# Places of float32r operands modulo 256 bytes in a three-stage kernel (MoE, state space, MoE)

## The reference

```python
x = x + 0.5 * ffn(layernorm(x))     # stage a
x = x + mamba(layernorm(x))         # stage m, which adds its own input too
x = x + 0.5 * ffn(layernorm(x))     # stage b, the same weights as stage a
```

## Time and profile before

| | |
|---|---|
| Runs of the kernel | 2362.97, 2363.86 and 2365.33 us, median 2363.86 |
| The profiled execution, from its first to its last instruction | 2361.8 us |
| TensorE busy with matmuls | 2295.3 us, 97% |
| TensorE busy loading weights | 2023.3 us, 86% |
| VectorE, ScalarE, GpSimd busy | 1371.3, 884.1, 690.8 us |
| Mean granted TensorE clock | 0.992 |

### The profile page before, as it was taken

How to read it: one execution, slowest core, us unless ns; L and a number is a source line. 1 busy time by engine, 2 the same in 40 slices (tenths; PEclk the granted TensorE clock), 3 DMA queues, 4 the chain that set the end, 5 groups by cost and what they waited for, 6 DMA issues and landing times.

```text
span 2361.8 us, 41282 instructions
## 1 busy us (share of the span) xinstructions
PE 2295.3 (97%) x16412; PEld 2023.3 (86%) x16412; DVE 1371.3 (58%) x3200; ACT 884.1 (37%) x1562; POOL 690.8 (29%) x534
## 2 busy tenths in 40 slices
PE   6999999999998999999999999999999999999997
PEld 6999998777788888888888888888999999777786
DVE  6767662222228777777777777778776763222221
ACT  5232221233327455554455555455322221233221
POOL 1244442112220332332332223231144444122121
PEclk9999999999999999999999999999999999999999
DMA  8876433989844111111111111104386622889948
GB/s 268 265 244 225 138 102 142 310 271 280 235 91 137 37 29 36 28 28 28 28 28 28 28 28 28 29 20 170 123 289 199 213 82 78 303 275 282 287 82 177
DMA packets 129279, 334.73 MB, mean 142 GB/s; under 512 B 24450, under 2 KB 45186, under 8 KB 118400
## 3 DMA queue, kind: packets, MB, share of 16 engines
q1 hardware_dynamic: 80592, 236.63, 28.2%
q0 software_dynamic: 48496, 95.46, 17.8%
HBM read 218.25 MB, written 172.77 MB: 166 GB/s over the span
## 4 chain that ended last, share of the span: by engine, by line
PE 87%; DMA 6%; DVE 4%; ACT 1%; issue 1%; DVEq 0%; POOL 0%; SPq 0%; ACTq 0%; POOLq 0%
PE m_p_ab L1666 4%; PE m_p_ab L1667 4%; PE m_p_ab L1668 4%; PE m_p_x L1668 3%; PE m_p_x L1667 3%; PE m_p_x L1666 3%; DMA out<-b_y,b_row_no 3%; PE p_up_a L757 3%; PE p_gate_a L757 3%; PE p_gate_a L758 2%; PE p_gate_a L759 2%; PE m_p_y L1786 2%; PE p_up_a L759 2%; PE p_up_a L758 2%; PE m_p_y L1787 2%; PE p_out_a L757 2%
## 5 line engine op out<-in xcount | busy, mean ns | idle before, releaser
L1982 DVE SCALAR_TENSOR_TENSOR m_xt<-m_ssm,m_convw,m_xt 128x256 f32<-128x256 f32 x384 | 219.0, 584 | 58.1 <-ACT m_ssm L1533 48.8
L495 POOL DMA_INDIRECT slot_rows<-a_hr,a_slot_now x128 | 128.3, 1002 | 147.0 <-PE p_gate_a L759 94.0
L495 POOL DMA_INDIRECT slot_rows<-b_hr,b_slot_now x128 | 128.5, 1004 | 146.2 <-PE p_gate_b L759 93.6
L1666 PE MATMUL m_p_ab<-m_ht_hi,m_wi_b_hi 128*128 128x256 f32 x576 | 161.5, 280 | 3.3 <-ACT m_ssm L1533 3.3
L1668 PE MATMUL m_p_ab<-m_ht_hi,m_wi_b_lo 128*128 128x256 f32 x576 | 159.6, 277 | 0.0
L1667 PE MATMUL m_p_ab<-m_ht_lo,m_wi_b_hi 128*128 128x256 f32 x576 | 159.5, 277 | 0.0
L757 PE MATMUL p_gate_a<-a_hts_hi,a_w_hi 128*128 128x256 f32 x512 | 150.2, 293 | 5.2 <-DVE a_hts_lo L1056 5.1
L757 PE MATMUL p_gate_b<-b_hts_hi,b_w_hi 128*128 128x256 f32 x512 | 148.0, 289 | 3.3 <-DVE b_hts_lo L1056 3.2
L1439 POOL TENSOR_TENSOR m_state_dec<-m_state,m_etot 128x1024 f32<-128x1024 f32 x31 | 74.0, 2387 | 255.2 <-ACT m_etot L1549 255.2
L757 PE MATMUL p_up_a<-a_hts_hi,a_w_hi 128*128 128x256 f32 x512 | 147.2, 288 | 0.0
L757 PE MATMUL p_up_b<-b_hts_hi,b_w_hi 128*128 128x256 f32 x512 | 147.1, 287 | 0.0
(11 more groups left out here) (376 smaller groups left out, 7372.3 us busy)
## 6 DMA issues: line engine op xcount, KB each, us to landing
a_ew<-in_ew SPq DMA_DIRECT2D x32, 1536.0 KB, 7.1
b_ew<-in_ew SPq DMA_DIRECT2D x32, 1536.0 KB, 7.2
after_ffn<-a_zeros POOLq DMA_DIRECT2D x6, 2048.0 KB, 9.3
out<-b_zeros POOLq DMA_DIRECT2D x6, 2048.0 KB, 10.2
slot_rows<-a_zeros POOLq DMA_DIRECT2D x1, 8336.0 KB, 39.6
a_rows<-slot_rows SPq DMA_DIRECT2D x32, 260.5 KB, 8.2
b_rows<-slot_rows SPq DMA_DIRECT2D x32, 260.5 KB, 8.2
m_x<-after_ffn SPq DMA_DIRECT2D x16, 512.0 KB, 3.6
```

Of the source, the lines that this page charges most:

```text
L495: g_.indirect_dma_start(out=xg, out_offset=bass.IndirectOffsetOnAxis(ap=slot_now[r % HR][:, at:at + 1], axis=0), in_=hr[r % HR][:, j, :], ...
L1666: t.matmul(out, l_hi, r_hi_, start=first, stop=False)
L1982: ins_ = v.scalar_tensor_tensor(xt[:, m, :], ssm[:, m, i:i + BM], convw[:, m, i:i + 1], xt[:, m, :], ALU.mult, ALU.add)
```

## The change

`Region` gets two arguments, `like` and `past`: a tile with them is moved up to the next place whose offset modulo 256 bytes is that of `like` plus `past`. With them, and with `HS_AT` and `ROUTED_AT` moved up by 96 and then 96 more bytes, streamed operands of 256 columns (`hts_hi`, `hts_lo`, `ht_hi`, `ht_lo`) lie 192 bytes past their weights modulo 256, which is to say the weights 64 bytes past them. The operands of products with 512 columns (`act_hi`, `act_lo`, `htr_hi`, `htr_lo` and `r_both`, `y_hi0`, `y_lo0`) lie at the same offset modulo 256 as their partners, and so do `wi_a_hi` and `wi_a_lo` with the shared weights' start. No instruction, wait or DMA is added, removed or moved in order; the tiles that follow a moved one get other addresses too.

```diff
-HS_AT = SHARED_AT + 4 * CI * (CONV - 1 + BM)
-ROUTED_AT = HS_AT + 4 * (10 * 1024 + 5 * TILES + 6 * TR)
+HS_AT = SHARED_AT + 8384
+ROUTED_AT = HS_AT + 41792
+LINE = 256
...
-    def __call__(self, name, shape, dt=F32):
+    def __call__(self, name, shape, dt=F32, like=None, past=0):
...
+        if like is not None:
+            self.next += (like + past - self.next) % LINE
         at = self.next
...
+        w_at, gap = c.first_byte, LINE - 64
...
-        hts_hi[0], hts_lo[0] = sb("hts_hi0", [P, KD, BS], F32R), sb("hts_lo0", [P, KD, BS], F32R)
+        hts_hi[0], hts_lo[0] = sb("hts_hi0", [P, KD, BS], F32R, w_at, gap), sb("hts_lo0", [P, KD, BS], F32R, w_at, gap)
...
-        hts_hi[1], hts_lo[1] = sb("hts_hi1", [P, KD, BS], F32R), sb("hts_lo1", [P, KD, BS], F32R)
-        act_hi, act_lo = sb("act_hi", [P, 2, 2, BS], F32R), sb("act_lo", [P, 2, 2, BS], F32R)
+        hts_hi[1], hts_lo[1] = sb("hts_hi1", [P, KD, BS], F32R, w_at, gap), sb("hts_lo1", [P, KD, BS], F32R, w_at, gap)
+        act_hi, act_lo = sb("act_hi", [P, 2, 2, BS], F32R, w_at), sb("act_lo", [P, 2, 2, BS], F32R, w_at)
...
-        r_both = rt("r_both", [P, KD, 2, E], F32R)
+        r_both = rt("r_both", [P, KD, 2, E], F32R, w_at)
...
-        htr_hi, htr_lo = rt("htr_hi", [P, 2, BR], F32R), rt("htr_lo", [P, 2, BR], F32R)
+        htr_hi, htr_lo = rt("htr_hi", [P, 2, BR], F32R, w_at), rt("htr_lo", [P, 2, BR], F32R, w_at)
...
-        wi_a = sb("wi_a_hi", [P, KD, SPLIT_COL - NH], F32R), sb("wi_a_lo", [P, KD, SPLIT_COL - NH], F32R)
+        w_at, gap = c.first_byte, LINE - 64
+        wi_a = (sb("wi_a_hi", [P, KD, SPLIT_COL - NH], F32R, w_at), sb("wi_a_lo", [P, KD, SPLIT_COL - NH], F32R, w_at))
...
-        ht_hi, ht_lo = sb("ht_hi", [P, KD, BM], F32R), sb("ht_lo", [P, KD, BM], F32R)
+        ht_hi, ht_lo = sb("ht_hi", [P, KD, BM], F32R, w_at, gap), sb("ht_lo", [P, KD, BM], F32R, w_at, gap)
+        sb.next += (w_at - sb.next) % LINE
...
+        sb = Region(nc, "m", c.first_byte + HS_AT)
         x[2], x[1] = sb("x2", [P, TM, D]), sb("x1", [P, TM, D])
```

## The result

The changed kernel takes 2340.4 us (median of 4 runs, 2337.7 to 2346.2), the kernel before 2363.4 us (median of 4): ratio 0.9907, 95% interval 0.989 to 0.9924. The forecast was 2327.5 us, with 2321 to 2334 us as its own range and 2311 to 2341 us as the outer one. The sign is right; 23 us came in place of 36.4, outside the forecast's own range and just within the outer one. The profiled execution spans 2337.9 us against 2361.8.

What follows compares the result with a forecast made beforehand. TensorE was taken to set the pace, except beside the experts and in the tail, where the adds' queue does. Savings 14.0 + 2.9 + 5.2 + 14.3 = 36.4 us from 2363.9 gave 2327.5 us, range 2321 to 2334, outer 2311 to 2341.

Steps and rivals of the forecast that it cites:

- That place counts, and the period of 256 bytes: All placed products: weights minus streamed operand, modulo 256 bytes, sets the distance of matmul starts; 64 suits 256 columns, 0 suits 512.
- The step of 114.0 ns for gate and up: Gate and up, runs of 48 between two down groups: mean step 114.0 ns, saving taken as 5.7 ns each.
- `wi_a` at 4.6 ns each: Stage m: 60 of a block's 72 wi_a products save 4.6 ns each, most of the 5.2 us for 16 blocks.
- `down` at 6.2 ns, `out_product` j = 0 at 2 ns: Products of 512 columns: down saves 6.2 ns each (bounds 5 and 7.3), out_product with j = 0 about 2 ns.
- The router's 7 ns: Stage a's 64 router products, mean 402 ns, go towards 391: some 7 ns each, 0.4 us in all.
- Stage a before the adds, 14.0 us: Units 1 to 39 with their downs and the router products save 10.7, 2.9 and 0.4 us, as TensorE sets the pace.
- The experts' stretch, put at a gain of 0: Beside the routed experts the adds set the pace; TensorE's 5.6 us are earned and given back in each stage.
- The tail at 0: End of stage b: blocks 14 and 15 would earn 2.9 us, the queue of adds cancels all but a fraction.
- Half: Rival, 10%: runs of 24 too short for the short pace, gate and up gain 2 ns, not 5.7; 2343 us.
- Everything counts: Rival, 10%: adds go faster with TensorE, so experts, tail and fourth part count too; 51.4 us gained, 2312 us.

## Why the prediction was right and wrong

- **That place counts, and the period of 256 bytes: right.** `wi_b` stayed at 277 ns though its rows moved by 256, and the cases at 256 and 320 bytes were as those at 0 and 64. The rule of the Trainium skill (TensorE: Matmul & The Clock Gate, Part 2, step 1), of two independent read ports, doesn't carry over to these products: 120.0 against 113.3 ns by the distance alone, with nothing else running.
- **The step of 114.0 ns for gate and up: this step failed.** The prediction put it as "(6 x 118 + 42 x 113.4) / 48 = 114.0 ns", six longer steps after which every run goes short. The rows it came from, 5 steps of 118 and then 113.4, were those of one entry into `wi_b`. Behind `down` with act at distance 0 nearly every run stays at 117.8 ns to its end (54 of 56; with TensorE alone 6 of 6). Measured: 116.5 ns, a saving of 3.2 in place of 5.7. The change put `down` at the distance where it is fastest itself, and that shuts gate and up out of their short pace; with act moved, 114.7 ns was measured.
- **`wi_a` at 4.6 ns each: the same failure.** 30 of its runs, all behind `out_product`, stayed at 117.8 ns (before 118.2). Stage m gained 2.6 us in place of 5.2.
- **`down` at 6.2 ns, `out_product` j = 0 at 2 ns: right.** Measured 5.5 for `down`, and 228.3 to 227.5 over both halves of `out_product`, some 1.5 for the one. The router's 7 ns were 3 (402 to 399). With hts alone undone, some 5 us are left for all of these.
- **Stage a before the adds, 14.0 us: 6.5.** TensorE's busy time fell by 8.4 us; most of what is missing is the pace above. 1.8 us more went into idle time, for which the sum had no term: TensorE now asks sooner for the router's rows, 8.3 us of waits in place of 6.2.
- **The experts' stretch, put at a gain of 0 because "The adds themselves do not change": right in part, and this step failed too.** The adds do go one after the other whatever TensorE does, and with TensorE 24 us less busy nothing was gained. But their transfers took 3.5 and 3.2 us less in the two stages (237.6 to 234.1 us in stage a). TensorE earned 3.8 us here, by the pace above, and not 5.6; 3.6 of them were kept, and the wait before block 14 stayed at 3.7 us in place of 9. The two errors are of opposite sign, so the total is nearer the forecast than its largest term.
- **The tail at 0: nearly right.** 1.2 us was gained behind block 10 of stage b. The last matmul came 27.5 us earlier, the last block add landed 23.9 us earlier, and the end came 23.9 us earlier, as it does if that queue sets the end.
- **The rivals.** "Half" was the nearest, at 2343 us and 10%: its size was right, its reason (runs of 24 too short) was not: more than half of the runs of 24 of gate and up did get short, of those of 48 behind `down` nearly none. "Everything counts" had a grain of truth in the adds, worth 3 us a stage; in stage b little of it reached the end.

## What to carry to other kernels

Read the distance of matmul starts run by run, with what stands before each run: a group's mean half way between two known values asks for that list. Don't place each product for itself; here a place of act that costs 1.4 ns more on each of 12 products of 512 columns turned the 48 behind them from 117.7 to 113.8 ns. Where a queue of read-modify-write transfers sets a stage, count a faster engine's gain there at no more than the few us by which the queue itself moves, and take that from a measurement.

## What was not expected of the hardware

- A series of float32r products with 256 columns holds one of two paces, 113.3 or 117.8 ns, for 48 and more products at one and the same distance (64 or 192), chosen by what ran before. Behind plain float32 products the choice changed with the absolute place as well. With the rows at 64, `down`'s operand at 0, 96 or 224 gives the longer one, at 32, 160 or 192 the shorter one.
- For 512 columns there is no such split at distance 0: 226.7 ns after some ten products; 228.8 at 192, 232.3 to 234.3 elsewhere.
- Both parts of a split operand must stand at the distance: with only one of them there the steps are 117.6 to 119.4 ns.
- Indirect adds of one queue, 128 rows each, take 4.6 to 10.8 us from issue to landing within one stretch. The same program's stretch was 264.0 us in one execution and 268.1 in another, and all of the difference lies in these times (234.1 and 238.3 us in sum).
